# Wh out of PSUM by ScalarE two banks at once, s rows spread by TensorE, first levels between the high parts

## What is computed

```python
Wh = x @ W
e = (Wh @ a1)[:, None] + (Wh @ a2)[None, :]           # s of the row plus t of the column
e = where(e > 0, e, 0.2 * e)
attention = softmax(where(adj > 0, e, -9e15), axis=1)
x = layernorm(x + elu(attention @ Wh))
n_x = concatenate([adj @ x / adj.sum(1), x], axis=1)
out = layernorm(x + n_x @ weight + bias)
```

## Time and profile before

| | |
|---|---|
| median of three runs | 1511.99 us |
| the profiled execution | 1511.81 us, its span 1509.8 us |
| TensorE busy | 1462.1 us (97%) |
| VectorE busy | 979.4 us (65%) |
| ScalarE busy | 970.4 us (64%) |
| GpSimd busy | 117.2 us (8%) |

### The profile page before, as it was taken

The page is one execution under the profiler, slowest core; times in us unless marked ns, Lnnn a source line. Parts: engine busy times, 40 slices in busy tenths (PEclk is TensorE's granted clock), DMA queues, the critical chain, the costliest instruction groups (busy, mean ns, idle before and its releaser), DMA issues.

```text
span 1509.8 us, 38620 instructions
## 1 busy us (share of the span) xinstructions
PE 1462.1 (97%) x14086; PEld 1298.6 (86%) x14086; DVE 979.4 (65%) x2781; ACT 970.4 (64%) x2384; POOL 117.2 (8%) x199
## 2 busy tenths in 40 slices
PE   7489999999999999999999999989999999999997
PEld 6378888888888888888888888878888898888886
DVE  7887877787787787788777777654343434444443
ACT  3699999999999999999999999921000000001000
POOL 1001100110010010010001000000000000000000
PEclk9699999999999999999999999999999999999998
DMA  9967998788878878868878880050000000000000
GB/s 170 113 73 82 118 106 96 83 91 96 87 86 97 92 82 97 94 81 95 94 85 90 95 93 21 12 144 15 17 17 17 17 17 17 17 17 14 17 17 18
DMA packets 99722, 101.70 MB, mean 67 GB/s; under 512 B 4704, under 2 KB 66912, under 8 KB 99680
## 3 DMA queue, kind: packets, MB, share of 16 engines
q0 software_dynamic: 33792, 67.11, 44.7%
q1 hardware_dynamic: 65888, 34.03, 9.9%
HBM read 289.77 MB, written 12.68 MB: 200 GB/s over the span
## 4 chain that ended last, share of the span: by engine, by line
PE 91%; ACT 3%; DVE 3%; DMA 1%; issue 1%; SPq 0%; POOL 0%; DVEq 0%; POOLq 0%
PE acc L623 57%; PE acc L698 30%; ACT level_ring L426 3%; PE turn_ps L724 2%; PE pack_ps L582 1%; PE turn_ps L712 1%; DVE words L771 1%; DVE wh_top L779 1%; DMA s_row<-s_and_t 1%; DMA s_and_t<-words 1%; ACT factors L474 0%; DMA factors<-in_x 0%; DVE edge_ring L905 0%; DVE level_ring L898 0%; ACT words L405 0%
## 5 line engine op out<-in xcount | busy, mean ns | idle before, releaser
L426 ACT ACTIVATE level_ring<-s_row,cols 128x256 fp8e4<-128x256 f32 x2048 | 832.5, 497 | 0.0
L623 PE MATMUL acc<-factors,edge_ring 128*128 128x258 f16 x4096 | 545.4, 274 | 20.4 <-DVE edge_ring L905 19.4
L623 PE MATMUL acc<-factors,level_ring 128*128 128x258 f16 x4096 | 544.8, 273 | 0.5 <-DVE row_sums L927 0.5
L698 PE MATMUL acc<-factors,adj_space 128*128 128x258 f16 x4096 | 463.6, 274 | 4.9 <-issue 4.9
L698 PEld LDWEIGHTS acc<-factors,adj_space 128*128 128x128 fp8e4 x4096 | 401.5, 98 | 56.1 <-issue 5.2
L623 PEld LDWEIGHTS acc<-factors,edge_ring 128*128 128x128 fp8e4 x4096 | 365.8, 97 | 67.1 <-issue 20.9
L623 PEld LDWEIGHTS acc<-factors,level_ring 128*128 128x128 fp8e4 x4096 | 364.8, 97 | 48.0 <-issue 0.9
L898 DVE TENSOR_TENSOR level_ring<-level_ring,edge_ring 128x1024 uint16<-128x1024 uint16 x256 | 174.4, 691 | 185.2 <-ACT level_ring L426 173.7
L524 ACT ACTIVATE part_sums<-acc 128x258 f32<-128x258 f32 x32 | 12.4, 386 | 294.5 <-PE acc L698 294.5
L582 PE MATMUL pack_ps<-pack_w,adj_space 128*128 128x32 bf16 x960 | 170.8, 178 | 0.0
L905 DVE TENSOR_TENSOR edge_ring<-edge_ring,level_ring 128x1024 uint16<-128x1024 uint16 x256 | 166.6, 683 | 0.0
(11 more groups left out here) (95 smaller groups left out, 691.8 us busy)
## 6 DMA issues: line engine op xcount, KB each, us to landing
adj_space<-in_adj POOLq DMA_DIRECT2D x64, 1024.0 KB, 17.2
x_parts<-parts SPq DMA_DIRECT2D x32, 129.0 KB, 5.2
factors<-x_parts SPq DMA_DIRECT2D x8, 516.0 KB, 6.5
factors<-in_x SPq DMA_DIRECT2D x8, 512.0 KB, 7.2
s_row<-s_and_t SPq DMA_DIRECT2D x32, 128.0 KB, 4.1
rows_x<-in_x SPq DMA_DIRECT2D x32, 128.0 KB, 2.1
x_rows<-rows_y SPq DMA_DIRECT2D x32, 128.0 KB, 9.8
rows_x<-x_rows SPq DMA_DIRECT2D x32, 128.0 KB, 2.1
```

What stands on the lines that cost most here:

```text
L426: a = act.activation(level_bytes[:, h % MASK_SLOTS, j, :], s_row[:, slot, :], ACT.Relu, bias=t_big[:, h * HALF + j:h * HALF + j + 1], scal ...
L623: m = pe.matmul(acc[a][:, 0:ROW], mask, factors[:, neg, jj, 0:ROW], start=(jj == 0), stop=(jj == NJ - 1))
L698: m = pe.matmul(acc[b][:, 0:ROW], ring_1_bytes[:, c, j, b * P:(b + 1) * P], factors[:, 0, jj, 0:ROW], start=(jj == 0), stop=(jj == NJ - 1))
```

## The change

- The four PSUM tensors `acc0` to `acc3` become one of four banks, so that one instruction can read two.
- VectorE's four copies a step become one, of s and t alone, from two banks (`copy_s_t`). ScalarE copies Wh, two banks in one instruction (`copy_wh`), one step behind its copy of the turned x and behind VectorE's small copy. TensorE waits for that before it writes the pair of banks again.
- `largest_wh` stands one step later in VectorE's list. The scaled t, one instruction over 64 columns before, is made in four of 16, three of them inside the loop.
- After step 2 TensorE multiplies the first four columns of s, each broadcast as a 128 x 128 tile, with the identity (`spread_s`), so that every partition has the 512 values of groups 0 and 1 in a PSUM bank. ScalarE copies them into `s_row` at step 4. The loads of s rows for groups 0 and 1 are gone; the store of s and t stays, for later groups.
- ScalarE's first 64 levels no longer wait for a load. Four stand right behind the loop, six behind the exponentials of t, and the rest, in pieces of 14, 16, 16 and 8, behind the two high parts of each chunk. The words of chunk 0 are copied ahead of the first high part.

```diff
-        acc = [ctx.enter_context(nc.psum_tensor(f"acc{k}", [P, 512], F32)) for k in range(2 * TPG)]
+        acc_banks = ctx.enter_context(nc.psum_tensor("acc", [P, 2 * TPG, 512], F32))
+        acc = [acc_banks[:, k, :] for k in range(2 * TPG)]
...
+        def wh_banks(k):
+            return acc_banks[:, 2 * (k % 2):2 * (k % 2) + 2, 0:2 * (F + 2)].rearrange("p h (j f) -> p h j f", j=2)
...
-            load_s(0, 0)
-            load_s(1, 1)
...
-            copy_turned(0)
-            for k in range(1, NX):
+            def copy_wh(k):
+                act.wait_ge(wh_ok, k + 1)
+                act.activation(wh[:, XB * k:XB * (k + 1), :].rearrange("p (h j) f -> p h j f", h=2),
+                               wh_banks(k)[:, :, :, 0:F], ACT.Copy).then_inc(wh_copied, 1)
+
+            def first_scores(j0, j1):
+                for j in range(j0, j1):
+                    if j % UNIT == 0:
+                        act.wait_ge(t_big_ok, j // UNIT + 1)
+                    a = act.activation(level_bytes[:, j // HALF, j % HALF, :], s_row[:, 0, :], ACT.Relu,
+                                       bias=t_big[:, j:j + 1], scale=-BIG, saturate=False)
+                    if j % HALF == HALF - 1:
+                        a.then_inc(score_ok, 1)
+
+            for k in range(NX):
                 copy_turned(k)
+                if k == 4:
+                    act.wait_ge(s_spread, 1)
+                    act.activation(s_row[:, :, :].rearrange("p k r -> p (k r)"), pack_ps[1][:, :], ACT.Copy)\
+                        .then_inc(s_row_ok, 1)
+                if k:
+                    copy_wh(k - 1)
+            copy_wh(NX - 1)
+            act.wait_ge(s_row_ok, 1)
+            first_scores(0, 4)
             act.wait_ge(s_turned, 1)
             act.activation(s_turn, turn_ps[0][:, 0:P], ACT.Copy).then_inc(s_turn_ok, 1)
...
-            act.wait_ge(t_big_ok, 1)
+            first_scores(4, 10)
...
+            copy_words(0, 0)
             for c in range(UPG):
                 for k in range(2):
                     act.wait_ge(product_ok, 2 * c + k + 1)
...
-                if c == 0:
-                    act.wait_ge(s_row_in[0], 16)
-                if c == 0:
-                    copy_words(0, 0)
-                for h in (2 * c, 2 * c + 1):
-                    scores(0, 0, h, True)
+                first_scores((10, 24, 40, 56)[c], (24, 40, 56, 64)[c])
                 if c < UPG - 1:
                     copy_words(0, c + 1)
...
                 if k >= 2:
-                    pe.wait_ge(wh_ok, k - 1)
+                    pe.wait_ge(wh_copied, k - 1)
...
+                if c == 1:
+                    pe.wait_ge(s_row_ok, 1)
...
+            def spread_s():
+                pe.wait_ge(wh_ok, 1)
+                for j in range(2 * TPG):
+                    m = pe.matmul(pack_ps[1][:, j * P:(j + 1) * P], s_col[:, j:j + 1].to_broadcast([P, P]), ident,
+                                  start=True, stop=True)
+                m.then_inc(s_spread, 1)
...
                 make_wh(k)
+                if k == 2:
+                    spread_s()
...
-            def copy_wh(k):
+            def copy_s_t(k):
                 dve.wait_ge(wh_made, k + 1)
-                j0 = XB * k
-                for half in range(2):
-                    bank = acc[2 * (k % 2) + half][:, 0:2 * (F + 2)].rearrange("p (j f) -> p j f", j=2)
-                    dve.tensor_copy(wh[:, j0 + 2 * half:j0 + 2 * half + 2, :], bank[:, :, 0:F])
-                    d = dve.tensor_copy(cols[:, 0:2, j0 + 2 * half:j0 + 2 * half + 2],
-                                        bank[:, :, F:F + 2].rearrange("p j k -> p k j"))
-                d.then_inc(wh_ok, 1)
+                dve.tensor_copy(cols[:, 0:2, XB * k:XB * (k + 1)].rearrange("p k (h j) -> p h j k", h=2),
+                                wh_banks(k)[:, :, :, F:F + 2]).then_inc(wh_ok, 1)
...
+            def scaled_t(c):
+                dve.wait_ge(wh_ok, XB * (c + 1))
+                js = slice(UNIT * c, UNIT * (c + 1))
+                dve.tensor_scalar(t_big[:, js], t_col[:, js], -BIG, None, ALU.mult).then_inc(t_big_ok, 1)
+
             for k in range(NX):
-                copy_wh(k)
-                if k < NX - 1:
-                    largest_wh(k)
+                copy_s_t(k)
+                if k:
+                    largest_wh(k - 1)
+                if k % XB == XB - 1 and k < NX - 1:
+                    scaled_t(k // XB)
```

More of the change, by code:

```diff
@@ L158, in adj_resnorm_kernel @@
         s_row_in = [sem("s_row_in0"), sem("s_row_in1")]
+        s_spread, s_row_ok, wh_copied = sem("s_spread"), sem("s_row_ok"), sem("wh_copied")
         rows_in, rows1_in = sem("rows_in"), sem("rows1_in")
@@ L179, in adj_resnorm_kernel @@
             sem(n) for n in "pos_copied neg_added nd_ok flag_ok full_ok inv_den_ok hidden_ok exp_in_ok exp_ok elu_ok".split())
-        y_ok, stats_ok, mv_ok, var_ok, rstd_ok, minus_ok, shift_ok, x1_ok, high_part, low_part = (
-            sem(n) for n in "y_ok stats_ok mv_ok var_ok rstd_ok minus_ok shift_ok x1_ok high_part low_part".split())
-        fill_ok, relu_ok, scaled_ok = sem("fill_ok"), sem("relu_ok"), sem("scaled_ok")
+        y_ok, stats_ok, mv_ok, var_ok, rstd_ok, x1_ok, high_part, low_part = (
+            sem(n) for n in "y_ok stats_ok mv_ok var_ok rstd_ok x1_ok high_part low_part".split())
         (low_ok, spread_ok, wide_ok, wh_saved, wh_out, w_t_in, w_wh_in, w_adj_in, w_x_in, w_stored, w_parts_in, w_step,
@@ L417, in _, with scores @@
             act.activation(f_col, t_col, ACT.Exp, bias=neg_ft, scale=ALPHA).then_inc(exp_cols_ok, 1)
-            act.wait_ge(t_big_ok, 1)
[L420 to L424, removed]
+            first_scores(4, 10)
+            def scores(g, slot, h):
+                act.wait_ge(mask_used, 8 * g + h + 1)
+                act.sem_inc(slot_free, 1)
                 for j in range(HALF):
@@ L452, in group @@
             def group(g, slot, loads, next_words, before_last=None, second=False):
-                act.wait_ge(s_row_in[slot], 16 * loads)
+                if not second:
+                    act.wait_ge(s_row_in[slot], 16 * loads)
                 for h in range(8):
@@ L488, in _ @@
                     act.activation(v_col, vy_col, ACT.Exp).then_inc(exp_cols_ok, 1)
-            group(1, 1, 1, {3: (1, 0)}, second=True)
-            group(2, 0, 2, {0: (1, 1), 1: (1, 2), 3: (1, 3)}, before_last=True)
-            group(3, 1, 2, {0: (2, 0), 1: (2, 1), 3: (2, 2)})
+            group(1, 1, 0, {3: (1, 0)}, second=True)
+            group(2, 0, 1, {0: (1, 1), 1: (1, 2), 3: (1, 3)}, before_last=True)
+            group(3, 1, 1, {0: (2, 0), 1: (2, 1), 3: (2, 2)})
             with act.Fori(2, NR - 1) as n:
-                group(PAIR * n, 0, n + 1, {1: (n, 3), 3: (n + 1, 0)})
-                group(PAIR * n + 1, 1, n + 1, {1: (n + 1, 1), 3: (n + 1, 2)})
-            group(NG - 2, 0, NR, {1: (NR - 1, 3)})
-            group(NG - 1, 1, NR, {})
+                group(PAIR * n, 0, n, {1: (n, 3), 3: (n + 1, 0)})
+                group(PAIR * n + 1, 1, n, {1: (n + 1, 1), 3: (n + 1, 2)})
+            group(NG - 2, 0, NR - 1, {1: (NR - 1, 3)})
+            group(NG - 1, 1, NR - 1, {})
             high_parts(NG - 2)
@@ L567, in make_wh @@
                 if k >= 2:
[L568 removed]
+                    pe.wait_ge(wh_copied, k - 1)
                 for j in range(XB):
[L570 to L571 removed]
+                    m = pe.matmul(wh_banks(k)[:, j // 2, j % 2, :], x_t[:, k % 2, j * P:(j + 1) * P], wq,
                                   start=True, stop=True)
@@ L640, in group @@
                         multiply(g, h, pack_chunk=pack_chunk)
+            pe.wait_ge(wh_copied, NX)
             pe.wait_ge(den_hi_ok, 4)
@@ L789, in _ @@
             largest_wh(NX - 1)
+            scaled_t(UPG - 1)
             dve.wait_ge(low_ok, 1)
@@ L823, in make_product @@
                 js = slice(c * UNIT, (c + 1) * UNIT)
+                if n == 0:
+                    dve.wait_ge(wh_copied, NX)
                 if n < 3:
```

5 lines of the change are left out of this document (1 added, 4 removed).

## The result

Six runs of the changed kernel took 1502.30 to 1504.06 us, median 1503.78; six of the kernel before beside them 1511.10 to 1513.19, median 1512.27. The ratio is 0.9941, with an interval of 0.9931 to 0.9951: faster by 8.5 us. The profiled execution took 1503.93 us, its span 1502.0. The forecast of 1504.3 us was right in size, but two errors of opposite sign are in it: group 1 starts 5.9 us earlier in the profiled pair, not 7.5, and 2.3 us were won behind the first pass, where I expected nothing.

A forecast was written before the change was run, and what follows sets the result against it. From 101.8 us TensorE is nearly gapless, so only the head and group 0 can gain; group 1 starting at 94.3 instead of 101.81 wins 7.5 us: 1511.81 - 7.5 = 1504.3 us, range 1502.2 to 1508.3.

The forecast's parts named there:

- The loop is paced by TensorE at 1.33 us: Loop over x: TensorE instead of VectorE sets the pace, 1.33 us a step instead of 1.52.
- 0.13 to spare over two steps: Loop over x: the chain through ScalarE takes 2.53 us per two steps, TensorE itself 2.66.
- the first rival: Loop paced by ScalarE: a two-bank copy of 1.1 us loses the loop's 2.8 us, giving 1507.1 us; chance 0.11.
- First product at 35.35: End of the head: the first product of factors moves from 37.53 to 35.35 us, 2.2 us won at the sign change.
- Group 0 on VectorE: Group 0: VectorE's list nearly without a gap; first multiply at 52.75 us instead of 59.16, chunk 2 at 78.47 instead of 84.90.
- The rival of stalls on VectorE: Group 0: waits for high parts and words replace today's stalls, leaving only the head's 2.2 us, 1509.6 us; chance 0.08.
- TensorE's clock: Group 0: today's clock loss kept for the pause of 4.5 us ahead of chunk 2; chunks 2 and 3 need 15.91 us.
- the rival of 1518.0: Group 0: TensorE's clock stays low over chunks 1, 2 and 3, 6.2 us later than today; chance 0.03.
- The other way, 1503.4: Group 0: no low clock behind the pause ahead of chunk 2; the gain grows by 0.9 us.
- From group 1 to the end each line is the same length: From group 1's first multiply on: TensorE's chain only moves along, nothing further won or lost.

The follow-up runs named there:

- banks_apart: Changed kernel with ScalarE's copy of Wh as two instructions, one for each bank; median 1504.19 us, ratio 0.995 to the kernel before.
- spread_only: Changed kernel with VectorE's four copies a step back, keeping TensorE's spread of s and the new order of levels; median 1507.81 us, ratio 0.9976 to the kernel before.
- loop_only: Changed kernel with s rows loaded from HBM again and ScalarE's first levels behind that load; median 1509.07 us, ratio 0.998 to the kernel before.
- words_late_warm: Changed kernel with each chunk's words copied behind its high parts and 30 idle multiplies ahead of chunk 2; median 1500.18 us, ratio 0.9923 to the kernel before.
- warm: Changed kernel with 40 idle multiplies on TensorE ahead of chunk 2 of group 0; median 1499.91 us, ratio 0.9923 to the kernel before.
- no_early: Changed kernel with no level ahead of the first high part, 16 behind each chunk's two; median 1506.14 us, ratio 0.9963 to the kernel before.

## Why the prediction was right

*The loop is paced by TensorE at 1.33 us:* right. The two-bank copy was 0.60, as taken, the spread 0.89, as taken. The step that was wrong is the margin, "0.13 to spare over two steps". The chain has the product start 0.05 behind ScalarE's row, but the product's weights are loaded 0.11 ahead of it (23.43 and 23.54), and that term is missing: 0.03 was left. banks_apart, with 0.06 more on ScalarE, went over the edge by every second step. So the first rival would have begun with a copy a few hundredths longer, not with one of 1.1 us, and that the loop stayed on TensorE's side by 0.03 was luck.

*First product at 35.35:* it came at 37.12. 1.19 of the 1.77 is the late start of this execution. The last small copy starts 0.2 later than that explains (32.60; I had 31.2). From there the maximum of step 14 and the scaled t cost less than was taken (32.60 to 34.19 is 1.59; 31.2 to 32.95 is 1.75). The other 0.5 is a gap that I did not foresee: VectorE stands 0.54 us ahead of line 854 with its operand there (the chain's "36.12 0.47 issue"). The gap, 0.53 to 0.54, is in every kernel with the copies on ScalarE, not in before nor in spread_only. Why it is there was not shown; it has about the size by which the change at group 1 is worth less than 7.5.

*Group 0 on VectorE:* right from the first product on. Product to first multiply 17.39 us (predicted 17.40), chunk 0 9.61 (9.72), ScalarE's wait 5.95 (5.8), VectorE's loss 1.22 (1.26), first multiply to chunk 2 25.61 (25.72), chunks 2 and 3 15.81 (15.91), no wait for the copied sums. The rival of stalls on VectorE (1509.6) fell with these rows, and loop_only shows what it would look like: with the s rows late, the waits take 0.6 of 2.0 us back.

*TensorE's clock:* it fell ahead of chunk 2 as taken over from before, and stayed full over chunk 1 and 3; the rival of 1518.0 fell. But the place of the low stretch is not fixed by the order of work alone: in loop_only, spread_only and words_late_warm it lies in chunk 1, behind pauses of 2.1 to 2.5 us (0.50 from 70.7 to 74.1 and from 68.6 to 72.0 in the first two). The other way, 1503.4, was tried as warm: 0.7 to 1.0 us at group 1, as its 0.9 says.

*From group 1 to the end each line is the same length:* wrong by 2.0 us. The first pass lost 0.30 (5.88 us earlier at group 1, 5.58 at its last multiply), of which about 0.26 is the loop, 0.02 a turn. From there on 2.27 us were won (510.46 less 508.19): 13 more multiplies in the first 30 us at a clock of 0.94 instead of 0.89, and some 0.9 at the end, where the clock was low for a shorter time too. That is chance and the place of code, not the change. With 1.2 us lost at the start it makes the agreement of 1503.93 with 1504.3 better than the reasoning deserved. The change's own part, measured in one clean stretch, is 7.1 us of 7.5.

## What to carry to other kernels

Ask which engine paces a loop before asking for a better instruction: moving a copy to an engine with room won 1.4 to 2.0 us by group 1, the same copy in one instruction instead of two 0.2 us in the loop. In a chain from engine to engine count the weight load ahead of a product too. A round trip through HBM for a few rows of values made ScalarE wait 5.89 us (loop_only) where a broadcast by TensorE costs 0.89, but the engine that waited must also have its list reordered, or part of the time returns as a wait later (0.7 us in no_early). Differences of one or two microseconds in one execution are judged from a fixed event to a fixed event, for pauses of TensorE end at different clocks from run to run.

## What the runs showed of the hardware

- ScalarE read 512 fp32 numbers from two PSUM banks in 0.60 us, as from one; two reads of 256 took 0.66.
- The weights of a product were loaded 0.11 us ahead of it in the changed kernel's loop (23.43 and 23.54), and at the earliest 0.05 behind the end of ScalarE's row that makes them (banks_apart). 0.03 us of delay at the load made every second step of banks_apart 1.36 us instead of 1.33.
- With pauses of 4.8 to 4.9 us between the passes the mean granted clock of 30 us from the last multiply of the first pass was 0.89 in some executions and 0.94 in others; before and the changed kernel differ there by 13 multiplies of 217 (1.4 us).
- Each pause of TensorE between the passes, in all thirteen profiles, ended 2.4 to 2.9 us behind the start of a 16 KB transfer on the queue that the profile calls "instruction".
- The gap at the jump of VectorE's loop was 0.50, 0.52 or 0.64 us for the same loop, and with 0.14 more of it the first pass from group 1 on was 1.85 us longer.
- Forty multiplies that never run put a second pause of TensorE (1.44 us) behind the eighth multiply of the second pass and made the way from the first pass to the end 2.7 us longer (510.92 against 508.19), a lower clock included.
